# Mixture-of-experts routing on one Trainium2 core: one-hot comparisons for eight row tiles at once in 16 bits, a shorter ranking chain, eight row slots, 71 blocks

## Chip, cores and metric

The kernel runs on one core of one Trainium2 chip. The metric is the device time of one execution, in microseconds (us). TensorE (PE) multiplies matrices, VectorE (DVE) and GpSimd (POOL) and ScalarE (ACT) work elementwise, SyncE (SP) issues most DMAs; they meet only at semaphores.

## What is computed

Six layers in turn act on 8192 tokens (8 sequences of 1024) of 128 numbers each: a gated mixture of experts (m0), a gated scan (s0), the same mixture again (m1), a second kind of mixture (m2), a selective scan (s1) and that mixture once more (m3). The change touches the four mixtures. What matters of the reference, for the second kind:

```python
capacity = int(CAP_RATIO * N * K / E) + 1          # 2561 rows per expert
k_probs, k_idx = jax.lax.top_k(probs, K)           # two of eight experts
flat_e = k_idx.reshape(-1)
onehot = jax.nn.one_hot(flat_e, E, dtype=jnp.int32)
rank = take_along_axis(cumsum(onehot, axis=0) - 1, flat_e[:, None], axis=1)[:, 0]
keep = rank < capacity
buf = zeros((E, capacity, H)).at[flat_e, slot].add(dispatched)
h = silu(einsum('ech,ehf->ecf', buf, w1));  out_buf = einsum('ecf,efh->ech', h, w2)
```

In the gated kind (m0, m1) no row is dropped, and an expert is `silu(x @ W1a + b1a) * (x @ W1b + b1b) @ W2 + b2`.

## The kernel before

All 8192 tokens stay in SBUF as 64 tiles of 128 rows (`c.x`), handled in 16 groups of four (`GRP`, `NG`). A mixture (`moe`) has two halves.

The first half is the routing. Per group, DVE computes the mean and variance, ACT normalises the four tiles into a slot of `xs` (L502; there are four slots, and ACT waits at L499 until the store of the group that had the slot has landed), SP stores the slot to `rows_in` in DRAM (L569), PE transposes it (L452) and computes eight logits per token (L458). SP issues its DMAs in program order: at group 2 (L584) it issues the loads of all expert weights before it stores that group. When the logits of all groups are there, DVE picks the two best experts (L337 to L349) and PE counts them with two 16-bit matmuls (L469, L470). Then comes the ranking (L366 to L412), a chain of short DVE instructions on 128x512 (all tokens by eight experts), 128x64 (all tokens) and 128x8 arrays, in which each waits for the one before (`link`). It gives each of the 16384 choices a row number: its rank within its expert plus the start of that expert, rounded up to blocks of 256 rows. Then the inverse is made (the sort loop, L416 to L427 and L472 to L487): for each group, 128x128 and 128x144 one-hot matrices in 32 bits are made of the low and high part of the row numbers, DVE making nine, ACT four and POOL three, and PE multiplies eight pairs of them into `src_ps`, where each row finds the token it comes from. There are two slots for the one-hot matrices, so a group waits until the group before the last has been multiplied (`marks_used`). After the loop DVE finds the expert of each block (L428 to L433) and writes the sources as integers (L436 to L442).

The second half runs over 72 blocks of 256 rows: POOL gathers the rows from DRAM (L636), PE transposes and multiplies them (L664, L670, L676, L686), DVE copies the block's expert weights (L760, L765), and the result goes back to DRAM, scattered to token order in m0 and m1 (L643) and by rows in m2 and m3 (L826). The number of blocks does not depend on the data; the ones beyond the last expert work on padding.

`add_and_store` (L1806) ends the program: POOL gathers the outputs of m3, DVE adds them, SP stores them.

## Time and profile before

The median of three runs is 3682.92 us (3680.77 to 3684.62). The profiled execution took 3686.03 us, with a span of 3683.9 us from the first to the last instruction.

| stage | us from the span's start | what it is |
|---|---|---|
| m0 routing | 12 to 157 | groups to 82, choice to 93, ranking to 108, sort loop to 156 |
| m0 blocks | 157 to 568 | PE busy 97% |
| m1 routing, blocks | 925 to 1078, to 1490 | as m0 |
| m2 routing, blocks | 1495 to 1675, to 1955 | groups fed by fetched rows of m1 |
| m3 routing, blocks | 3095 to 3235, to 3515 | as m2, without the fetches |
| end | 3518 to 3684 | gather, add, store |

| engine | busy us | share of the span |
|---|---|---|
| PE | 2759.8 | 75% |
| DVE | 2230.1 | 61% |
| POOL | 2187.1 | 59% |
| ACT | 1574.8 | 43% |

The chain that ended last leads back only through the last stage. All layers follow one another behind barriers, so each stage has to be read by itself. In the rows below, a number in square brackets is the idle time of the engine before the instruction, and behind the arrow stands what ended it.

### The profile page before, as it was taken

How to read it: one execution, taken by the hardware profiler on the slowest of the kernel's cores; microseconds unless marked ns; L12 is line 12 of the kernel's file. 1: busy time of each engine (PE TensorE's matmuls, PEld its weight loads, DVE VectorE, ACT ScalarE, POOL GpSimd, SP SyncE). 2: the span in 40 equal slices, each digit the busy share in tenths (PEclk: the TensorE clock that was granted, in tenths of full speed). 3: DMA queues.
4: the chain of work that ended last, by engine and by line, in shares of the span. 5: the costliest groups of instructions: out<-in, count | busy, mean ns of one | idle time of the engine just before them, and what ended most of it. 6: DMA issues, size and time to landing. Idle time of an engine off the chain costs nothing. (4 is left out here: it accounts for less than half of the span.)

```text
span 3683.9 us, 48898 instructions
## 1 busy us (share of the span) xinstructions
PE 2759.8 (75%) x13060; PEld 2000.6 (54%) x13064; DVE 2230.1 (61%) x4405; ACT 1574.8 (43%) x2906; POOL 2187.1 (59%) x1931
## 2 busy tenths in 40 slices
PE   4699995998569999348995567767867865599910
PEld 4599983444459898348993223323322323589910
DVE  3766653555375565584331698999989987733322
ACT  4433334553443333243333566456556633433300
POOL 0577771321057777335553888988988684455567
PEclk9999997888589999569997799899999998699955
DMA  6011122000401111512222678778877875022222
GB/s 166 11 47 47 46 43 57 23 23 0 121 10 47 45 47 44 149 35 53 70 69 52 222 268 284 257 266 277 274 256 271 277 258 187 23 57 71 69 67 78
DMA packets 287279, 430.21 MB, mean 117 GB/s; under 512 B 58620, under 2 KB 196639, under 8 KB 287168
## 3 DMA queue, kind: packets, MB, share of 16 engines
q1 hardware_dynamic: 251328, 357.61, 29.5%
q0 software_dynamic: 35840, 71.39, 8.3%
q8 instruction: 37, 0.61, 0.1%
q14 instruction: 74, 0.61, 0.1%
HBM read 368.04 MB, written 62.91 MB: 117 GB/s over the span
## 5 line engine op out<-in xcount | busy, mean ns | idle before, releaser
L636 POOL DMA_INDIRECT m_rows<-rows_in,m_source x576 | 560.3, 973 | 370.1 <-PE m_T_ps L664 217.8
L1516 PE MATMUL s_y_ps<-s_prod,ident 128*128 128x512 f32 x1024 | 550.6, 666 | 277.2 <-DVE s_prod L1785 276.9
L1778 DVE TENSOR_TENSOR_SCAN s_dA<-s_dA,s_dBu 128x1024 f32<-128x1024 f32 x256 | 586.2, 2290 | 143.6 <-POOL s_dBu L1476 70.8
L1476 POOL TENSOR_TENSOR s_dBu<-s_du,s_B_row 128x1024 f32<-128x1024 f32 x256 | 602.6, 2358 | 101.8 <-DVE s_dA L1778 94.1
L670 PE MATMUL m_A_ps<-m_rowsT,m_own 128*128 128x256 f32 x2304 | 576.8, 383 | 2.0 <-ACT m_rowsT L718 1.1
L686 PE MATMUL m_Y_ps<-m_own,m_hid 128*128 128x128 f32 x4608 | 562.2, 275 | 3.6 <-issue 3.6
L686 PEld LDWEIGHTS m_Y_ps<-m_own,m_hid 128*128 128x128 f32 x4608 | 537.3, 192 | 5.7 <-issue 5.6
L1516 PEld LDWEIGHTS s_y_ps<-s_prod,ident 128*128 128x128 f32 x1024 | 192.3, 205 | 598.1 <-DVE s_prod L1785 404.9
L670 PEld LDWEIGHTS m_A_ps<-m_rowsT,m_own 128*128 128x128 f32 x2304 | 420.3, 193 | 49.4 <-ACT m_rowsT L718 1.9
L1606 ACT ACTIVATE s_dA<-s_delta,s_decay 128x1024 f32<-128x1024 f32 x256 | 285.6, 1118 | 337.4 <-DVE s_prod L1785 330.8
L728 ACT ACTIVATE m_act_a<-m_A_ps,m_own 128x256 f32<-128x256 f32 x576 | 241.4, 470 | 434.9 <-PE m_A_ps L670 303.4
L643 POOL DMA_INDIRECT rows_by_token<-m_y_sb,m_target x288 | 307.2, 1067 | 138.3 <-issue 100.9
L777 DVE SCALAR_TENSOR_TENSOR m_hid<-m_B_ps,m_own,m_act_a 128x256 f32<-128x256 f32 x576 | 250.7, 476 | 179.9 <-ACT m_act_a L728 165.4
L1785 DVE TENSOR_TENSOR s_prod<-s_dA,s_C_row 128x1024 f32<-128x1024 f32 x256 | 313.3, 1224 | 8.3
L733 ACT ACTIVATE m_hid<-m_A_ps 128x512 f32<-128x512 f32 x288 | 171.9, 597 | 329.4 <-PE m_A_ps L670 329.4
L676 PE MATMUL m_B_ps<-m_rowsT,m_own 128*128 128x256 f32 x1152 | 297.4, 381 | 0.0
L760 DVE COPY m_own<-m_packs 128x1032 f32 (+1 forms) x288 | 170.1, 591 | 127.2 <-issue 76.2
L791 DVE COPY m_y_sb<-m_Y_ps 128x256 f32<-128x256 f32 x144 | 61.2, 425 | 294.6 <-PE m_Y_ps L686 294.6
L676 PEld LDWEIGHTS m_B_ps<-m_rowsT,m_own 128*128 128x128 f32 x1152 | 220.1, 191 | 30.3
L477 PE MATMUL m_src<-m_is_high,m_is_low 128*128 128x144 f32 x1024 | 151.9, 306 | 100.0 <-DVE m_is_high L424 90.0
L477 PEld LDWEIGHTS m_src<-m_is_high,m_is_low 128*128 128x128 f32 x1024 | 139.2, 203 | 115.4 <-DVE m_is_high L424 87.3
L551 POOL COPY m_low_now<-m_low 128x4 f32 (+1 forms) x64 | 12.2, 191 | 309.8 <-DVEq L414 280.9
(228 smaller groups left out, 3994.4 us busy)
## 6 DMA issues: line engine op xcount, KB each, us to landing
s_B_row<-s_bc_rows SPq DMA_DIRECT2D x256, 512.0 KB, 5.3
s_C_row<-s_bc_rows SPq DMA_DIRECT2D x256, 512.0 KB, 5.4
rows_out<-m_y_sb SPq DMA_DIRECT2D x144, 128.0 KB, 1.8
rows_in<-m_xs SPq DMA_DIRECT2D x64, 256.0 KB, 2.3
m_rows<-rows_in,m_source POOLq DMA_INDIRECT x576
s_got<-rows_by_token SPq DMA_DIRECT2D x16, 512.0 KB, 5.2
m_got<-rows_by_token SPq DMA_DIRECT2D x32, 256.0 KB, 4.1
rows_by_token<-m_y_sb,m_target POOLq DMA_INDIRECT x288, 2.3
```

What stands on the lines that cost most here:

```text
L477: ins = nc.tensor.matmul(src_ps[:, :], is_low[:, slot, j % 2, j // 2, :], is_high[:, slot, j, :], start=isinstance(g, int) and g == 0 and ...
L636: pool.indirect_dma_start(rows[:, b % 2, r, :], None, c.rows_in, bass.IndirectOffsetOnAxis(source[:, 2 * b + r:2 * b + r + 1], 0)).then_in ...
L643: pool.indirect_dma_start(c.rows_by_token, bass.IndirectOffsetOnAxis(target[:, 2 * b + r:2 * b + r + 1], 0), y_sb[:, b % 2, r, :], None, b ...
L670: ins = nc.tensor.matmul(A_ps[h][:, j, :], own[:, slot, W1A + f * P:W1A + (f + 1) * P], rowsT[:, slot, :], start=True, stop=True)
L676: ins = nc.tensor.matmul(B_ps[h][:, j, :], own[:, slot, W1B + f * P:W1B + (f + 1) * P], rowsT[:, slot, :], start=True, stop=True)
L686: ins = nc.tensor.matmul(Y_ps[slot][:, r, :], hid[:, slot, f, at(r, P)], own[:, slot, W2 + f * D:W2 + (f + 1) * D], start=(f == 0), stop=( ...
L777: ins = nc.vector.scalar_tensor_tensor(out=hid[:, slot, f, :], in0=B_ps[h][:, j, :], scalar=own[:, slot, B1B + f:B1B + f + 1], in1=act_a[: ...
L1476: nc.gpsimd.tensor_tensor(dBu[q % RING][:, :], du[s % 2][:, h, :], B_row[q % RING][:, :], ALU.mult).then_inc(dBu_ready, 1)
L1516: ins = nc.tensor.matmul(y_ps[:, at(cc, 512)], c.ident[:, :], prod[q % 2][:, at(cc, 512)], start=(n == 0), stop=(n == NS - 1))
L1606: nc.scalar.activation(dA[q % 2][:, :], delta[s % 2][:, h, :], ACT.Exp, scale=decay[:, h, n:n + 1]).then_inc(dA_ready, 1)
L1778: nc.vector.tensor_tensor_scan(dA[q % 2][:, :], dA[q % 2][:, :], dBu[q % RING][:, :], 0.0, ALU.mult, ALU.add).then_inc(scanned, 1)
L1785: nc.vector.tensor_tensor(prod[q % 2][:, :], dA[q % 2][:, :], C_row[q % RING][:, :], ALU.mult).then_inc(prod_ready, 1)
```

## The change

- Slots of `xs`: eight in place of four (`DEEP`).
- Counting: the order of the moving operand is by expert and then tile, read with a step of eight 16-bit elements; the matrix `earlier` holds -1 so that the sum of the two gives the rank.
- Ranking: one scan over all experts that starts anew where `restart` is zero, in place of eight; the start of the expert is added before the choice is picked, so that two instructions per choice go; both choices are split into low and high part together. In m2 and m3 a dropped choice gets a number from 32768 on, which matches no row; `keep`, the weights and the row to fetch back are worked out after the sort loop.
- Sort loop: `is_high` and `is_low` of eight tiles are one DVE instruction each (1152 and 1024 elements per partition, 16 bits, the tile innermost). A one-hot matrix no longer carries the token number; `is_high` is multiplied by the tile number (DVE in even groups, POOL in odd ones) and by the row within the tile (ACT). PE multiplies with 288 columns, both parts together, reading both operands with a step of eight 16-bit elements. The loop is written out. Afterwards the two parts are put together by two more DVE instructions.
- Blocks: 71 in place of 72, which is still enough for any split of the choices.
- Constants are made at the start for the new shapes (1024 and 1152 elements per partition where there were 128 and 144).

```diff
-NBLK = 2 * TOK // BLK + E
+NBLK = (2 * TOK + E * (BLK - 1)) // BLK
 ROWS = NBLK * BLK
 CAP = int(1.25 * TOK * 2 / E) + 1
+DROPPED = 32768.0
...
-            link(nc.gpsimd.memset(c.before[:, :], 1.0))
-            link(nc.gpsimd.affine_select(out=c.before[:, :], in_=c.before[:, :], compare_op=ALU.is_gt,
-                                         fill=0.0, base=0, pattern=[[1, P]], channel_multiplier=-1))
+            link(nc.gpsimd.memset(c.earlier[:, :], 0.0))
+            link(nc.gpsimd.affine_select(out=c.earlier[:, :], in_=c.earlier[:, :], compare_op=ALU.is_gt,
+                                         fill=-1.0, base=0, pattern=[[1, P]], channel_multiplier=-1))
...
+            link(nc.gpsimd.memset(c.restart[:, :, :], 1.0))
+            link(nc.gpsimd.memset(c.restart[:, :, 0:1], 0.0))
...
-            link(nc.gpsimd.iota(low_i[:, :], pattern=[[1, P]], base=0, channel_multiplier=0))
-            link(nc.gpsimd.iota(high_i[:, :], pattern=[[P, ROWS // P]], base=0, channel_multiplier=0))
-            link(nc.gpsimd.iota(code_i[:, :, :], pattern=[[TOK, 2], [P, NT]], base=1, channel_multiplier=1))
+            link(nc.gpsimd.iota(low_i[:, :, :], pattern=[[1, P], [0, 2 * GRP]], base=0, channel_multiplier=0))
+            link(nc.gpsimd.iota(high_i[:, :, :], pattern=[[1, ROWS // P], [0, 2 * GRP]], base=0, channel_multiplier=0))
+            link(nc.gpsimd.iota(tile_i[:, :, :, :], pattern=[[GRP, NG], [NT, 2], [1, GRP]], base=0, channel_multiplier=0))
...
+        DEEP = 8
         with ExitStack() as rc:
             def rsb(name, shape, dt=F32):
                 return rc.enter_context(nc.sbuf_tensor(f"{tag}_{name}", shape, dt))
-            xs = rsb("xs", [P, 4, GRP, D])
+            xs = rsb("xs", [P, DEEP, GRP, D])
...
+            is_low = rsb("is_low", [P, 2, P, 2 * GRP], BF16)
+            is_high = rsb("is_high", [P, 2, ROWS // P, 2 * GRP], BF16)
+            coded = rsb("coded", [P, 2, 2, ROWS // P, 2 * GRP], BF16)
...
-            src_ps = rc.enter_context(nc.psum_tensor(f"{tag}_src", [P, ROWS // P], F32))
+            src_ps = rc.enter_context(nc.psum_tensor(f"{tag}_src", [P, 2, ROWS // P], F32))
...
-                for e in range(E):
-                    link(nc.vector.tensor_tensor_scan(cum[:, e, :], c.ones_f[:, :], tot3[:, :, e], 0.0,
...
+                link(nc.vector.tensor_tensor_scan(cum[:, :, :].rearrange("p e t -> p (e t)"), c.restart[:, :, :].rearrange("p e t -> p (e t)"),
+                                                  tot_ps[:, :], 0.0, ALU.mult, ALU.add))
                 if gated:
-                    link(nc.vector.tensor_copy(cnt[:, :], cum[:, :, NT - 1]))
+                    link(nc.vector.tensor_scalar(cnt_i[:, :], cum[:, :, NT - 1], float(BLK - 1), None, ALU.add))
                 else:
-                    link(nc.vector.tensor_scalar(cnt[:, :], cum[:, :, NT - 1], float(CAP), None, ALU.min))
...
+                    link(nc.vector.tensor_scalar(cnt_i[:, :], cum[:, :, NT - 1], float(CAP), float(BLK - 1), ALU.min, ALU.add))
+                link(nc.vector.tensor_tensor(cum[:, :, :], cum[:, :, :], by_expert[0], ALU.add))
                 link(nc.vector.tensor_scalar(cnt_i[:, :], cnt_i[:, :], BLK.bit_length() - 1, BLK.bit_length() - 1,
                                              ALU.logical_shift_right, ALU.logical_shift_left))
                 link(nc.vector.tensor_copy(cnt[:, :], cnt_i[:, :]))
                 link(nc.vector.tensor_tensor_scan(run_end[:, :], c.ones_f[:, 0:E], cnt[:, :], 0.0, ALU.mult, ALU.add))
                 link(nc.vector.tensor_tensor(run_base[:, :], run_end[:, :], cnt[:, :], ALU.subtract))
+                if not gated:
+                    link(nc.vector.tensor_scalar(over[:, :, :], cum[:, :, :], float(CAP), DROPPED, ALU.is_ge, ALU.mult))
+                    link(nc.vector.tensor_tensor(cum[:, :, :], cum[:, :, :], over[:, :, :], ALU.add))
+                link(nc.vector.tensor_tensor(place[:, :, :], cum[:, :, :].rearrange("p e t -> p t e"),
+                                             run_base[:, :].unsqueeze(1).to_broadcast([P, NT, E]), ALU.add))
                 for k in range(2):
-                    link(nc.vector.tensor_tensor(t8[:, :, :], oh[k][:, :, :], u8[:, :, :], ALU.mult))
-                    link(nc.vector.tensor_reduce(rank[:, :], t8[:, :, :], AX.X, ALU.add))
...
+                    link(nc.vector.tensor_tensor(t8[:, :, :], oh[k][:, :, :], place[:, :, :], ALU.mult))
+                    link(nc.vector.tensor_reduce(pos[:, k, :], t8[:, :, :], AX.X, ALU.add))
+                link(nc.vector.tensor_copy(pos_i[:, :, :], pos[:, :, :]))
+                link(nc.vector.tensor_scalar(high_i[:, :, :], pos_i[:, :, :], P.bit_length() - 1, None, ALU.logical_shift_right))
+                link(nc.vector.tensor_scalar(low_i[:, :, :], pos_i[:, :, :], P - 1, None, ALU.bitwise_and))
+                link(nc.vector.tensor_copy(high[:, :, :, :], high_i[:, :, :].rearrange("p k (g j) -> p g k j", j=GRP)))
+                link(nc.vector.tensor_copy(low[:, :, :, :], low_i[:, :, :].rearrange("p k (g j) -> p g k j", j=GRP)))
+                def spread_over(v, n):
+                    return v.rearrange("p k j -> p (k j)").unsqueeze(1).to_broadcast([P, n, 2 * GRP])
+                for g in range(NG):
+                    wait(dve, marks_used, g - 1)
+                    nc.vector.tensor_tensor(is_high[:, g % 2, :, :], c.high[:, :, :], spread_over(high[:, g, :, :], ROWS // P),
+                                            ALU.is_equal).then_inc(high_ready, 1)
+                    nc.vector.tensor_tensor(is_low[:, g % 2, :, :], c.low[:, :, :], spread_over(low[:, g, :, :], P),
+                                            ALU.is_equal).then_inc(low_ready, 1)
+                    if g % 2 == 0:
+                        dve.wait_ge(high_ready, g + 1)
+                        nc.vector.tensor_tensor(coded[:, g % 2, 0, :, :], is_high[:, g % 2, :, :],
+                                                spread_over(c.tile_code[:, g, :, :], ROWS // P), ALU.mult).then_inc(tiles_coded[0], 1)
+                if not gated:
+                    for k in range(2):
+                        link(nc.vector.tensor_scalar(keep[:, :], pos[:, k, :], DROPPED, None, ALU.is_lt))
+                        link(nc.vector.tensor_tensor(weight[k][:, :], weight[k][:, :], keep[:, :], ALU.mult))
                 for k in range(2):
-                    link(nc.vector.tensor_copy(low[k][:, :], put_i[k][:, :]))
-                    link(nc.vector.tensor_scalar(put_i[k][:, :], put_i[k][:, :], bits, bits,
...
+                    link(nc.vector.tensor_scalar(get_i[k][:, :], pos[:, k, :], float(ROWS - 1), None, ALU.min))
...
+                value, code, second, padding = (found[:, i, :] for i in range(4))
+                link(nc.vector.tensor_scalar(value, src_ps[:, 0, :], float(P), None, ALU.mult))
+                link(nc.vector.tensor_tensor(value, value, src_ps[:, 1, :], ALU.add))
+                link(nc.vector.tensor_scalar(code, value, -1.0, 0.0, ALU.add, ALU.max))
+                link(nc.vector.tensor_scalar(second, code, float(TOK), float(-TOK), ALU.is_ge, ALU.mult))
...
-                ch = chosen[:, :, :].rearrange("p t e -> p (t e)")
-                nc.tensor.matmul(pre_ps[:, :], c.before[:, :], ch, start=True, stop=True)
...
+                ch = chosen[:, :, :].rearrange("p t e -> p e t")
+                nc.tensor.matmul(by_expert[0], c.earlier[:, :], ch, start=True, stop=True)
+                nc.tensor.matmul(by_expert[1], c.ones_bf[:, :], ch, start=True, stop=True).then_inc(counted, 1)
+                for g in range(NG):
+                    pe.wait_ge(low_ready, g + 1)
+                    pe.wait_ge(tiles_coded[g % 2], g // 2 + 1)
+                    pe.wait_ge(rows_coded, g + 1)
                     for j in range(2 * GRP):
-                        ins = nc.tensor.matmul(src_ps[:, :], is_low[:, slot, j % 2, j // 2, :], is_high[:, slot, j, :],
-                                               start=isinstance(g, int) and g == 0 and j == 0,
-                                               stop=last and j == 2 * GRP - 1)
+                        ins = nc.tensor.matmul(src_ps[:, :, :], is_low[:, g % 2, :, j], coded[:, g % 2, :, :, j],
+                                               start=(g == 0 and j == 0), stop=(g == NG - 1 and j == 2 * GRP - 1))
                     ins.then_inc(marks_used, 1)
-                sort(0, 0)
-                sort(1, 1)
...
...
-                    wait(act, transposed, g - 3)
-                    wait(act, xs_stored[g % 4], g // 4 * 16)
+                    wait(act, transposed, g - DEEP + 1)
+                    wait(act, xs_stored[g % DEEP], g // DEEP * 16)
...
-                act.wait_ge(parts_known, 1)
...
+                for g in range(NG):
+                    act.wait_ge(high_ready, g + 1)
+                    nc.scalar.activation(coded[:, g % 2, 1, :, :], is_high[:, g % 2, :, :], ACT.Copy,
+                                         scale=c.row_code[:, 0:1]).then_inc(rows_coded, 1)
...
-                pool.wait_ge(parts_known, 1)
...
+                for g in range(1, NG, 2):
+                    pool.wait_ge(high_ready, g + 1)
+                    nc.gpsimd.tensor_tensor(coded[:, 1, 0, :, :], is_high[:, 1, :, :],
+                                            c.tile_code[:, g, :, :].rearrange("p k j -> p (k j)").unsqueeze(1).to_broadcast([P, ROWS // P, 2 * GRP]),
+                                            ALU.mult).then_inc(tiles_coded[1], 1)
...
-                with pe.Fori(0, (NBLK - 4) // 2) as i:
+                with pe.Fori(0, (NBLK - 3) // 2) as i:
                     step(i * 2 + 2, 0)
                     step(i * 2 + 3, 1)
-                step(NBLK - 2, 0)
-                step(NBLK - 1, 1, last=True)
-                down(NBLK - 1, 1)
+                step(NBLK - 1, 0, last=True)
+                down(NBLK - 1, 0)
```

## Rows read from the trace of the kernel before

**Rows 1.** Busy time by stage: start:end, length, engines, PEclk granted, DMA share, GB/s.

```profile
93.10:108.40 15.30, 0.00 (x0) 0.00 (x0) 13.87 (x38) 0.04 (x1) 0.01 (x1) 1.00 0.00 0
...
3095.00:3168.30 73.30, 42.60 (x207) 41.25 (x206) 38.22 (x192) 37.36 (x91) 27.77 (x64) 0.52 0.40 115
```

**Rows 2.** ACT in order of time: start, us, what; m0, m1, m2, m3.

```profile
53.76 1.65 ACT L502 ACTIVATE m_xs<-x_res,m_shift,m_rstd 128x128 f32<-128x128 f32 x4 [21.43 <-DMA rows_in<-m_xs]
...
974.46 1.65 ACT L502 ACTIVATE m_xs<-x_res,m_shift,m_rstd 128x128 f32<-128x128 f32 x4 [20.97 <-DMA rows_in<-m_xs]
...
984.27 1.65 ACT L502 ACTIVATE m_xs<-x_res,m_shift,m_rstd 128x128 f32<-128x128 f32 x4 [0.48 <-DVE m_shift L300]
...
1541.70 1.65 ACT L502 ACTIVATE m_xs<-x_res,m_shift,m_rstd 128x128 f32<-128x128 f32 x4 [12.93 <-DVE m_own_shift L304]
...
3125.27 1.65 ACT L502 ACTIVATE m_xs<-x_res,m_shift,m_rstd 128x128 f32<-128x128 f32 x4 [8.04 <-DMA rows_in<-m_xs]
```

**Rows 3.** SP's queue in order of time, m1.

```profile
944.73 14.32 SPq L182 DMA_DIRECT2D m_packs<-in_L_ffn_W  x4
...
969.70 28.52 SPq L569 DMA_DIRECT2D rows_in<-m_xs  x14
```

**Rows 4.** DVE in order of time, m2's groups.

```profile
1538.89 2.31 DVE L275 SCALAR_TENSOR_TENSOR x_res<-m_got,weight,x_res 128x128 f32<-128x128 f32 x8 [10.36 <-DMA m_got<-rows_by_token]
```

**Rows 5.** DVE in order of time, ranking and first one-hot, m0 then m2.

```profile
93.12 2.53 DVE L367 TENSOR_TENSOR_SCAN m_cum<-ones_f,m_tot 128x64 f32<-128x64 f32 x8
...
97.13 1.03 DVE L372 TENSOR_TENSOR m_u<-m_u,m_cum 128x512 f32<-128x512 f32 x1
...
98.41 0.17 DVE L378 TENSOR_SCALAR m_cnt<-m_cnt 128x8 f32<-128x8 f32 x1
...
99.64 0.69 DVE L386 TENSOR_TENSOR m_t<-m_oh,m_u 128x512 f32<-128x512 f32 x1
...
108.41 0.29 DVE L421 TENSOR_SCALAR m_is_low<-low,m_low 128x128 f32<-128x128 f32 x1
...
1607.76 2.53 DVE L367 TENSOR_TENSOR_SCAN m_cum<-ones_f,m_tot 128x64 f32<-128x64 f32 x8
...
1626.17 0.29 DVE L421 TENSOR_SCALAR m_is_low<-low,m_low 128x128 f32<-128x128 f32 x1
```

**Rows 6.** DVE at the end of m0's sort loop and at the first block.

```profile
154.43 0.31 DVE L436 TENSOR_SCALAR m_is_high<-m_src 128x144 f32<-128x144 f32 x1
...
157.59 0.70 DVE L760 COPY m_own<-m_packs 128x1032 f32 x1 [1.56 <-issue]
```

**Rows 7.** PE in m0's sort loop, last group; x16 are eight matmuls.

```profile
151.72 2.23 PE L477 MATMUL m_src<-m_is_high,m_is_low 128*128 128x144 f32 x16 [0.27 <-DVE m_is_high L424]
```

**Rows 8.** All engines in order of time, one step of s1.

```profile
3039.33 1.22 DVE L1785 TENSOR_TENSOR s_prod<-s_dA,s_C_row 128x1024 f32<-128x1024 f32 x1
3039.47 2.35 POOL L1476 TENSOR_TENSOR s_dBu<-s_du,s_B_row 128x1024 f32<-128x1024 f32 x1 [1.00 <-DVE s_dA L1778]
3040.47 2.29 DVE L1778 TENSOR_TENSOR_SCAN s_dA<-s_dA,s_dBu 128x1024 f32<-128x1024 f32 x1
...
3040.61 1.98 PE L1516 MATMUL s_y_ps<-s_prod,ident 128*128 128x512 f32 x4 [1.23 <-DVE s_prod L1785]
...
3040.65 1.12 ACT L1606 ACTIVATE s_dA<-s_delta,s_decay 128x1024 f32<-128x1024 f32 x1 [2.34 <-DVE s_prod L1785]
```

**Rows 9.** PE groups by line: xcount, busy us, mean ns, idle before.

```profile
L470 PE MATMUL m_tot<-m_chosen,ones_bf 128*128 128x512 bf16 x4 | 2.5, 634 | 48.2 <-DVE m_chosen L349 48.2
```

**Rows 10.** PE in order of time, two blocks of m0, two of m3.

```profile
501.19 0.38 PE L664 MATMUL m_T_ps<-ident,m_rows 128*128 128x128 f32 x2
...
506.65 0.38 PE L664 MATMUL m_T_ps<-ident,m_rows 128*128 128x128 f32 x2
...
3440.13 0.38 PE L664 MATMUL m_T_ps<-ident,m_rows 128*128 128x128 f32 x2
...
3443.86 0.38 PE L664 MATMUL m_T_ps<-ident,m_rows 128*128 128x128 f32 x2
```

164 lines of the change are left out of this document (45 added, 119 removed).

## The prediction

> **What bounds the kernel now.** I began with the busy slices of the page. They show PE near full in four stretches (the blocks of the mixtures) and no engine full in the routing ahead of each. The chain that ended last reaches back only through the last stage, which the change leaves alone, so I asked for the busy time by stage. In the ranking only DVE works, 13.87 of 15.30 us, and the DMA engines do nothing [rows 1]: whatever is cut from that chain comes off the end. The instructions in order of time then gave the rest. ACT, which sets the pace of the groups, stood still for 21.43 us in m0, 20.97 in m1 and 8.04 in m3 until a store of an older group had landed [rows 2]; SP had queued that store behind the weight loads [rows 3]. In m2 ACT waited 12.93 us for DVE instead, and DVE 10.36 us for fetched rows [rows 2, 4]. The sort loop takes 154.43 - 108.41 = 46.0 us from its first one-hot to the first closing instruction, on DVE, ACT, POOL and PE together [rows 5, 6]. In the blocks PE sets the pace.
>
> **Eight slots.** ACT does a group in (984.27 - 974.46) / 4 = 2.45 us [rows 2]. With four slots it stops after group 5, because group 6 needs the slot of group 2, whose store waits behind the loads. With eight it stops after group 9: four more groups, 9.8 us, move under the wait in m0 and in m1, and 11 us of the wait remain there, since the loads are no faster. In m3 the wait was 8.04 us, less than four groups, so all of it goes. Behind the waiting ACT instruction are the copies for PE, so PE moves with it. In m2 the wait is another one and nothing is gained. The stores then come in a burst; SP issued 14 in 28.52 us [rows 3], which was still at ACT's pace, so I cost the burst at nothing; if a store took over 2.45 us, it would show as a new ACT wait. Sum: 9.8 + 9.8 + 8.0 = 27.6 us less.
>
> **Ranking.** An instruction on 512 elements takes 0.69 us and one on 8 takes 0.17; with the step to the next I count 0.73 and 0.21. Reading across the experts makes the 0.69 a 1.03 [rows 5]. Eight scans of 64 take 2.53 us, one of 1024 takes 2.29 [rows 5, 8]; between the two, one of 512 takes 1.22. The new chain in m0: scan 1.25, five small ones 1.05, the add of the counts 0.73, the place with its crossing read 1.07, four on 512 elements 2.92, and five on 128 elements, for which I take 0.30 each by the 0.31 of a 144-element one [rows 6], 1.5. That is 8.5 us against 108.41 - 93.12 = 15.3: 6.8 us less. In m2 and m3 two more on 512 elements make it 10.0, against 1626.17 - 1607.76 = 18.4 [rows 5]: 8.4 less. All on the path. Sum: 2 x 6.8 + 2 x 8.4 = 30.4 us less.
>
> **Sort loop.** *DVE.* No row has a two-input instruction on 16-bit operands. At one element per step it follows the 0.69 for 512 and 1.22 for 1024 [rows 5, 8], so 1.36 us for 1152 elements. The fast end is the copy that took 0.70 us for 1032 elements [rows 6], so 0.76 for 1152 and 0.69 for 1024. The two-input row moves four bytes of each operand in a step; 1152 elements of two bytes that lie side by side are 576 such words, and that lands on the fast end. I take it: `is_high` 0.79 with its step, `is_low` 0.72, the multiplication in even groups 0.79.
>
> *POOL.* In odd groups it multiplies 1152 elements. By 2.35 us for 1024 [rows 8] that is 2.65. It could be as little as 1.26, which is ACT's rate [rows 8], if 16 bits help there.
>
> *PE.* A group was eight matmuls in 16 pieces in 2.23 us, so 0.129 us a piece of 144 columns at two cycles each [rows 7]. A 16-bit matmul on 512 columns took 0.634 us [rows 9] where the granted clock was near half [rows 1]; at 1.2 GHz two cycles a column would be 0.85, so 16-bit columns take one. A matmul of 288 columns then costs the same 0.129 and a group 1.2 us. But each column is now read 16 bytes from the last. The only price of such a read is DVE's 1.03 for 0.69 [rows 5], which without the 0.16 of fixed cost is 1.64 times per element. I take that: 0.206 us a matmul, 1.8 us a group. One cycle gives 1.2, two cycles 2.15.
>
> *The period.* An odd group can start only when the odd group before it has been multiplied. So two groups take at least `is_high` 0.76 + POOL 2.65 + PE 1.8 + three handovers. DVE to POOL took 0.17 (a scan ended at 3039.30, POOL began at 3039.47) and DVE to PE 0.06 (3040.55 to 3040.61) [rows 8]; 0.3 in all. That is 5.5 us. DVE needs 3.8 for its five instructions and PE 3.3; ACT needs 1.26 for each group, by 1.12 for 1024 [rows 8], and ends before POOL. The first odd group starts 2.3 us in, the last is multiplied after 2.3 + 8 x 5.5 = 46.3 us. DVE's work behind the loop fits under that in m0 and m1; in m2 and m3 the weights that were moved behind it end at 46.6. Before, it was 46.0 in m0 and as much elsewhere within 0.3 us. So the loop gains nothing by this sum, and two more closing instructions at 0.34 [rows 6] add 0.7: 1.0 us more per stage, 4.0 in all. The loop's other end: with one cycle a column the period is 4.9, and 18 us less in all; with two it is 5.86, and 12 more.
>
> *Beside the sum.* DVE's product and scan of s1, with two SBUF inputs each, ran during POOL's multiplication, and that took 2.35 us all the same [rows 8]. The Trainium skill (SBUF — State Buffer, "SBUF: two separate sides") says that such a DVE instruction and a GpSimd one that reads SBUF exclude each other for the whole instruction; the trace does not agree, and the rule is a rival below. And by the page VectorE: DVE Perf Modes, "The perf-mode tier table", 16-bit `tensor_tensor` runs at two elements per cycle, an estimate of 0.75 us for 1152; no row here shows that.
>
> **The rest.** Blocks: one less at 506.65 - 501.19 = 5.46 us in m0 and m1 and 3443.86 - 3440.13 = 3.73 in m2 and m3 [rows 10], 18.4 us less. Counting: two matmuls now read with a step; by the 1.64 above each adds 0.27 us at 1.2 GHz, partly under the weights that DVE works out meanwhile; I take 1 us in all, 0 to 2. The constants grow by two arrays of some 1100 elements on POOL and DVE, an estimate of 3 to 5 us in a row, under the first load of tokens; 0, up to 1 if that cover is short.
>
> **Sum.** -27.6 - 30.4 + 4.0 - 18.4 + 1 = -71.4 us. Against the profiled 3686.03 that is 3614.6; the median of the runs lies 3.1 lower, so 3611.5.
>
> **Rivals.**
> - POOL is faster in 16 bits (1.26): period 4.1, 10 us less per stage, 3571. Nothing in the trace speaks for it.
> - DVE makes one element per step. Then DVE sets the period, 2 x 1.39 + 2 x 1.26 + 1.39 = 6.7, and a stage takes 10.6 more: 3654. For it: every two-input row here has that rate.
> - DVE and POOL exclude each other: 3.8 + 2.65 = 6.5 per pair, 8 more per stage, 3643. Against it: [rows 8].
> - The slots bring nothing, because the stores, bunched, hold ACT again: 3639.
> - Slower than before: the stepped read costs PE the time, not the ratio, that it costs DVE. (1.03 - 0.16) / 512 = 1.7 ns an element [rows 5] is 0.49 us for 288 columns, 0.5 a matmul, and PE sets the period: 16 x 0.5 = 8.0 us. The loop takes 66.3, 20 more in each stage: 3691.5. It decides from 0.48 us a matmul on. For it: this is the only stepped read in the trace. Against it: PE's clock and port are others. The Trainium skill (SBUF — State Buffer, "Specifications (TRN2)") has lines of 16 bytes that want two hits each for full bandwidth, and each column here is a line of its own; it gives no size, and no row of PE shows one.
>
> **How the numbers follow.** Forecast 60% (3593 to 3623 with the ends of the stepped read); faster POOL 9%; DVE at one per step 9%; exclusion 8%; slots without effect 7%; slow stepped read 7%. The range 3575 to 3652 takes in the forecast, the exclusion, the slots and the near halves of two others. 0.2%, about what a measurement can tell from no change, is 7.4 us: only the last rival gets there, so faster 93%, the same 2%, slower 5%.
>
> **What would show it.** ACT's wait for the store at 11 us in m0 and m1 and gone in m3; 8.5 and 10.0 us from the scan to the first `is_high`; `is_high` at 0.76; POOL's product at 2.65; a matmul of the sort loop each 0.13 (one cycle), 0.21 or 0.25; two groups in 5.5 us, POOL's product in every chain; 71 blocks. The prediction is wrong if DVE idles in the loop for PE rather than for POOL's groups, or if `is_high` takes 1.36.

## The result: 0.4% slower, and the profile after

The changed kernel takes 3697.02 us (median; 3692.5 to 3699.8) beside 3682.19 us of the kernel before on the same chip: ratio 1.0037, 95% interval 1.0025 to 1.0049. The profiled execution took 3695.92 us, its span 3694.1 us, so 10.2 us more span than the 3683.9 of before. I had forecast 71.4 us less.

First the busy time by stretch: the sort loop of m0 before the change, then the four sort loops after it, each from the first one-hot instruction to the first closing instruction (columns: stretch; length; busy time of PE, PEld, DVE, ACT and POOL with the count of instructions; granted clock as a share of the full 2.4 GHz; DMA share; GB/s).

```profile
108.40:154.40 46.00, 37.66 (x256) 34.49 (x256) 42.59 (x153) 30.39 (x80) 33.44 (x64) 1.00 0.00 0
```

```profile
92.32:159.60 67.28, 64.99 (x128) 18.58 (x128) 31.53 (x52) 19.89 (x16) 19.68 (x8) 1.00 0.00 0
1012.04:1079.34 67.30, 65.02 (x128) 18.55 (x128) 31.55 (x51) 19.89 (x16) 19.71 (x8) 0.50 0.00 0
1619.57:1686.86 67.29, 65.00 (x128) 18.58 (x128) 32.38 (x56) 19.88 (x16) 19.69 (x8) 0.50 0.00 0
3180.20:3247.47 67.27, 64.99 (x128) 18.55 (x128) 32.38 (x56) 19.89 (x16) 19.69 (x8) 0.50 0.00 0
```

Three things matter. A loop takes 67.3 us, where before it took 46.0 [rows 5, 6]. PE is busy for 65.0 of them, DVE for less than half, POOL for less than a third; before, DVE was the busiest. And the first loop ran at a granted clock of 1.00 (2.4 GHz), the other three at 0.50 (1.2 GHz), and they are equally long: what PE does here does not go by its clock. A matmul costs 64.99 / 128 = 0.508 us, 1.79 ns for each of 284 columns.

The groups by line say the same from the other side (busy us, mean ns of one; then the idle time before them and what ended it), first PE's group of the kernel before, then those of the changed kernel:

```profile
L477 PE MATMUL m_src<-m_is_high,m_is_low 128*128 128x144 f32 x1024 | 151.9, 306 | 100.0 <-DVE m_is_high L424 90.0
```

```profile
L464 PE MATMUL m_src<-m_coded,m_is_low 128*128 128x284 bf16 x512 | 260.0, 687 | 44.5 <-ACT m_coded L507 44.5
...
L398 DVE TENSOR_TENSOR m_is_high<-high,m_high 128x1136 bf16<-128x1136 bf16 x64 | 48.0, 749 | 134.7 <-PE m_src L464 134.6
...
L457 PE MATMUL m_tot<-m_chosen,ones_bf 128*128 128x512 bf16 x4 | 4.3, 1078 | 0.0
```

DVE stands still for 134.6 us ahead of `is_high`, for PE. Before, the counting matmul of 512 columns took 634 ns [rows 9]; now that its operand is read across the experts, 16 bytes from one column to the next, it takes 1078 ns (the other counting matmul 1060). The mean of one sort matmul, 687 ns, is longer than the 508 from one to the next, since they overlap.

Single instructions in order of time, DVE and POOL in m0 (start, us, instruction; in brackets the idle time before it), and ACT's wait for a slot in m0 and m1:

```profile
94.92 0.68 DVE L400 TENSOR_TENSOR m_is_low<-low,m_low 128x1024 bf16<-128x1024 bf16 x1
98.77 0.75 DVE L398 TENSOR_TENSOR m_is_high<-high,m_high 128x1136 bf16<-128x1136 bf16 x1 [3.17 <-PE m_src L464]
...
152.26 2.46 POOL L520 TENSOR_TENSOR m_coded<-m_is_high,tile_code 128x1136 bf16<-128x1136 bf16 x1 [5.65 <-DVE m_is_high L398]
...
152.69 2.30 DVE L412 TENSOR_SCALAR get<-m_pos 128x64 int32<-128x64 f32 x2
...
159.60 0.30 DVE L421 TENSOR_SCALAR m_found<-m_src 128x142 f32<-128x142 f32 x1 [1.75 <-PE m_src L464]
```

```profile
54.15 1.65 ACT L481 ACTIVATE m_xs<-x_res,m_shift,m_rstd 128x128 f32<-128x128 f32 x4 [12.01 <-DMA rows_in<-m_xs]
...
973.87 1.65 ACT L481 ACTIVATE m_xs<-x_res,m_shift,m_rstd 128x128 f32<-128x128 f32 x4 [11.77 <-DMA rows_in<-m_xs]
```

`is_high` on 1136 elements takes 0.75 us: the fast end that I took, where one element per step would be 1.36. The waits for a store fell from 21.43 and 20.97 us [rows 2] to 12.01 and 11.77, and the one of m3 is gone. Also, two short `TENSOR_SCALAR` of 64 elements lasted 2.30 us together, beside POOL's product, where such an instruction took 0.20 in the kernel before; the experiments on GpSimd beside VectorE take that up.

Where the 10.2 us come from, by the same five points in both traces (start of the logits' copy, scan, first one-hot, first closing instruction, first copy of the blocks), summed over m0, m1, m2 and m3 (us; the forecast of +1.2 for the loops is the 4.0 of the sum less the 2.8 of the closing instructions):

| stretch | before | after | difference | forecast |
|---|---|---|---|---|
| all outside the routing (slots, blocks) | | | -46.8 | -27.6 - 18.4 |
| logits to scan (counting) | 51.9 | 54.3 | +2.4 | +1 |
| scan to first one-hot (ranking) | 67.4 | 35.4 | -32.0 | -30.4 |
| the four sort loops | 184.7 | 269.1 | +84.5 | +1.2 |
| closing | 10.8 | 12.9 | +2.1 | +2.8 |
| sum | | | +10.2 | -71.4 |

All of the miss is in one line of the table.

### The profile page after: what moved, and what is told of

It is laid out like the page before. It is cut to its first block and busy times, and to the rows that moved or that the text cites. A ratio compares the mean times of both kernels' runs of the same rounds, so it can differ in the third digit from the quotient of the medians.

```text
span 3694.1 us, 45149 instructions
## 1 busy us (share of the span) xinstructions
PE 2844.7 (77%) x12432; PEld 1913.7 (52%) x12432; DVE 2150.1 (58%) x3886; ACT 1525.3 (41%) x2634; POOL 2129.3 (58%) x1697
## 5 line engine op out<-in xcount | busy, mean ns | idle before, releaser
L601 POOL DMA_INDIRECT m_rows<-rows_in,m_source x568 | 552.0, 972 | 372.3 <-PE m_T_ps L629 211.4
L635 PE MATMUL m_A_ps<-m_rowsT,m_own 128*128 128x256 f32 x2272 | 567.1, 382 | 2.1 <-ACT m_rowsT L682 1.1
L651 PE MATMUL m_Y_ps<-m_own,m_hid 128*128 128x128 f32 x4544 | 554.4, 275 | 3.6 <-issue 3.6
L651 PEld LDWEIGHTS m_Y_ps<-m_own,m_hid 128*128 128x128 f32 x4544 | 529.8, 192 | 5.7 <-issue 5.6
L520 POOL TENSOR_TENSOR m_coded<-m_is_high,tile_code 128x1136 bf16<-128x1136 bf16 x32 | 78.8, 2462 | 397.8 <-DVE m_is_high L398 397.8
L464 PE MATMUL m_src<-m_coded,m_is_low 128*128 128x284 bf16 x512 | 260.0, 687 | 44.5 <-ACT m_coded L507 44.5
L464 PEld LDWEIGHTS m_src<-m_coded,m_is_low 128*128 128x128 bf16 x512 | 74.3, 146 | 233.4 <-issue 181.7
```

Source lines behind the costliest of these rows:

```text
L464: ins = nc.tensor.matmul(src_ps[:, :, :], is_low[:, g % 2, :, j], coded[:, g % 2, :, :, j], start=(g == 0 and j == 0), stop=(g == NG - 1 a ...
L601: pool.indirect_dma_start(rows[:, b % 2, r, :], None, c.rows_in, bass.IndirectOffsetOnAxis(source[:, 2 * b + r:2 * b + r + 1], 0)).then_in ...
L635: ins = nc.tensor.matmul(A_ps[h][:, j, :], own[:, slot, W1A + f * P:W1A + (f + 1) * P], rowsT[:, slot, :], start=True, stop=True)
L651: ins = nc.tensor.matmul(Y_ps[slot][:, r, :], hid[:, slot, f, at(r, P)], own[:, slot, W2 + f * D:W2 + (f + 1) * D], start=(f == 0), stop=( ...
```

## The experiments

Theory: the read of the moving operand with a step of 16 bytes sets the pace of the sort loop. Rivals: the matmuls are slow for another reason (two-part destination, unrolled code, waits); or the step of the weights is what costs; and, within the theory, whether the price goes by column, by instruction, or by bytes passed over. Eight of the runs below (all but those of halves, 32 bytes, 32-bit inputs, the changed kernel again and the two stretches) were on two other chips, on which the kernel before takes 3841 and 3845 us, so there ratios are compared, not times. Six runs were a single execution each: weights in pairs, 32-bit inputs, halves, 32 bytes and the two stretches; of them the traces are read, not the times.

**Pairs instead of eights.** The one-hot tensors are laid out so that PE steps over 4 bytes; the vector work is the same. `WL` and `WH` are the tiles side by side in `is_low` (the weights) and in `coded` (the moving operand); the cut shows `is_low` and the matmul alone.

```
+WL, WH = 2, 2
...
-            is_low = rsb("is_low", [P, 2, P, 2 * GRP], BF16)
+            is_low = rsb("is_low", [P, 2, 2 * GRP // WL, P, WL], BF16)
...
-                        ins = nc.tensor.matmul(src_ps[:, :, :], is_low[:, g % 2, :, j], coded[:, g % 2, :, :, j],
+                        ins = nc.tensor.matmul(src_ps[:, :, :], is_low[:, g % 2, j // WL, :, j % WL], coded[:, g % 2, :, j // WH, :, j % WH],
```

> The changed kernel with its one-hot tensors laid out in pairs of tiles instead of eights (the innermost dimension is 2): the vector instructions write as many elements in as many instructions, and TensorE reads both operands with a step of 4 bytes where it was 16. Theory 1 (the matmuls are slow by the 16-byte step): a matmul falls from 0.508 us to 0.12 to 0.24 us (284 columns at either clock level), the period of two groups becomes 0.75 + 2.46 + 8 x 0.2 + 0.3 = 5.1 us instead of 8.1, each stage's loop about 42 us instead of 67.3, and the time is 3697 - 4 x 25 = 3597 us. Theory 2 (it is not the step: 16-bit matmuls into a destination of two parts, the unrolled code, or the waits ahead of each group make them slow): nothing changes in a matmul, 3697 us. A third outcome: the vector instructions lose two elements per cycle with so short an innermost dimension: is_high takes 1.2 us instead of 0.75.

Measured: ratio 0.9802 (0.9786 to 0.9818), where the changed kernel has 1.0037. The groups of this kernel:

```profile
L465 PE MATMUL m_src<-m_coded,m_is_low 128*128 128x284 bf16 x512 | 110.4, 384 | 101.0 <-ACT m_coded L508 54.0 <-POOL m_coded L521 47.0
...
L399 DVE TENSOR_TENSOR m_is_high<-high,m_high 128x1136 bf16<-128x1136 bf16 x64 | 80.3, 1255 | 22.4 <-PE m_src L465 21.7
```

PE's 260.0 us became 110.4, and it now waits for the others. So the layout alone is worth 2.4%, and theory 2 falls. But the loops take 45.5 to 46.5 us, not 42, and `is_high` has a mean of 1255 ns instead of 749. That is not the loss of two elements per cycle that I had as a third outcome: most of them take 0.74 us, and some far longer. The order of time shows which (PE's eight matmuls of a group among them):

```profile
105.20 2.05 PE L465 MATMUL m_src<-m_coded,m_is_low 128*128 128x284 bf16 x8 [0.74 <-ACT m_coded L508]
...
105.78 2.46 POOL L521 TENSOR_TENSOR m_coded<-m_is_high,tile_code 128x1136 bf16<-128x1136 bf16 x1 [2.61 <-DVE m_is_high L399]
...
107.29 1.56 DVE L399 TENSOR_TENSOR m_is_high<-high,m_high 128x1136 bf16<-128x1136 bf16 x1 [0.99 <-PE m_src L465]
...
110.43 0.75 DVE L399 TENSOR_TENSOR m_is_high<-high,m_high 128x1136 bf16<-128x1136 bf16 x1 [0.32 <-PE m_src L465]
...
111.26 2.46 POOL L521 TENSOR_TENSOR m_coded<-m_is_high,tile_code 128x1136 bf16<-128x1136 bf16 x1 [3.02 <-DVE m_is_high L399]
...
112.19 2.13 DVE L399 TENSOR_TENSOR m_is_high<-high,m_high 128x1136 bf16<-128x1136 bf16 x1 [0.41 <-PE m_src L465]
...
113.82 1.19 PE L465 MATMUL m_src<-m_coded,m_is_low 128*128 128x284 bf16 x8 [1.67 <-POOL m_coded L521]
...
115.51 0.74 DVE L399 TENSOR_TENSOR m_is_high<-high,m_high 128x1136 bf16<-128x1136 bf16 x1
```

The first of these POOL products ends at 108.24, the comparison at 108.85; the second ends at 113.72, the comparison at 114.32. Both comparisons end 0.6 us after POOL's product, whatever their start: they wait for its end. The one at 110.43, with POOL idle, takes 0.75. In the changed kernel no `is_high` is longer than 0.75 us, because PE kept DVE waiting for longer.

How much of the 45.5 us is that wait? POOL's products begin 5.48 or 5.07 us apart (105.78, 111.26, 116.32), so two groups take about what the sum of the prediction had, 5.5 us, with no wait in it. The longer periods are those in which PE's group took 2.05 us, at a granted clock of 0.50: POOL's product, PE's group and the next `is_high` follow one another there, and the held comparison lies beside them. In the shorter ones PE took 1.19 us, at 1.00, and was done at 115.01, but `is_high` began only at 115.51, behind the DVE instructions that the held comparison had put off. By this the wait costs under 0.5 us in about half of the periods, an estimate of 2 us a loop; what holds the loop is POOL's product, 2.46 us in every two groups.

**Which operand.** Only the moving operand in pairs, then only the weights.

```
-WL, WH = 2, 2
+WL, WH = 8, 2
```

> As the changed kernel, but only the moving operand (coded, with is_high) is laid out in pairs, so a step of 4 bytes; the weights (is_low) are still read with a step of 16 bytes. If the step of the moving operand costs the time (my theory: 284 columns against 128 in the weights, and the weight load, 146 ns each, lies beside the matmul before it): as with both in pairs, a matmul of 0.12 to 0.24 us, about 3597 us. If the step of the weights costs it: 0.508 us a matmul as before, 3697 us.

```
-WL, WH = 2, 2
+WL, WH = 2, 8
```

> The other half: only the weights (is_low) in pairs, a step of 4 bytes, the moving operand (coded) still with a step of 16 bytes. Theory of the moving operand: 0.508 us a matmul as in the changed kernel, 3697 us. Theory of the weights: 0.12 to 0.24 us a matmul, about 3597 us.

Measured: 0.9805 (0.9789 to 0.9821) and loops of 45.6 to 47.1 us for the moving operand alone; for the weights alone loops of 66.5 us and one time of 3848.0 us beside 3841.4. The moving operand is nearly the whole of it: PE is busy for 117.1 us with it alone in pairs, for 110.4 with both and for 256.9 with the weights alone, so the step of the weights is worth 3 to 7 us in 512 matmuls, about 0.01 us each.

**How the price grows.** Fours, a step of 8 bytes:

```
-WL, WH = 2, 2
+WL, WH = 4, 4
```

> Both operands laid out in fours: a step of 8 bytes. If the cost grows with the bytes stepped over, a matmul lies midway, 0.25 to 0.33 us, the period is 0.75 + 2.46 + 8 x 0.29 + 0.3 = 5.8 us, the loop about 48 us, the time 3697 - 4 x 19 = 3620 us. If it is a threshold at 16 bytes, 0.12 to 0.24 us and about 3597 us as with pairs; if any step costs the full price, 0.508 us and 3697 us.

Measured: 0.9843 (0.9826 to 0.9859). Busy time by stretch, its first and third loop:

```profile
93.26:140.98 47.72, 33.99 (x128) 14.76 (x128) 38.86 (x51) 19.88 (x16) 19.68 (x8) 0.78 0.00 0
1719.87:1768.56 48.69, 33.97 (x128) 14.87 (x128) 39.70 (x55) 19.89 (x16) 19.67 (x8) 0.61 0.00 0
```

33.99 / 128 = 0.266 us a matmul, 0.93 ns a column, at both mixes of the clock: midway, as by the bytes passed over, not a threshold. The pairs did go by the clock, 1.19 / 8 = 0.149 us at 1.00 and 2.05 / 8 = 0.256 at 0.50. So a step of 8 bytes nearly doubles a matmul at the full clock and adds next to nothing at half of it.

**Columns or instructions; 32 bytes.** Two matmuls of 142 columns each for one of 284; and `coded` spread to 32 bytes a column.

```
-                        ins = nc.tensor.matmul(src_ps[:, :, :], is_low[:, g % 2, :, j], coded[:, g % 2, :, :, j],
+                        for half in range(2):
+                            ins = nc.tensor.matmul(src_ps[half][:, 0:ROWS // P], is_low[:, g % 2, :, j], coded[:, g % 2, half, :, j],
```

> The changed kernel (step of 16 bytes) with each matmul of 284 columns made as two of 142, into two banks: twice the instructions, the same columns. If the stepped read costs its time per column (1.79 ns): 0.254 us each, the group still 4.06 us, the loop 67.3 us, no change. If it is a cost of each instruction (a table of descriptors, a restart of the read): 0.5 us each, 8.1 us a group, loops of 130 us, 250 us more.

```
-            coded = rsb("coded", [P, 2, 2, ROWS // P, 2 * GRP], BF16)
+            coded = rsb("coded", [P, 2, 2, ROWS // P, 4 * GRP], BF16)
```

> The changed kernel with coded spread out so that TensorE's columns lie 32 bytes apart instead of 16 (the eight values of a column and then eight unused ones); is_high, is_low and the number of columns as they were. The pairs, fours and eights gave 0.149, 0.264 and 0.508 us for 284 columns, 0.52, 0.93 and 1.79 ns a column at steps of 4, 8 and 16 bytes. If the time follows the bytes passed over: 3.6 ns a column, 1.02 us a matmul, 8.1 us a group, loops of 130 us and 250 us more. If it stops growing once each column has 16 bytes of its own: 0.508 us, the loop 67.3 us, no change but for the vector writes.

Measured, the matmul groups of the two:

```profile
L465 PE MATMUL m_src<-m_coded,m_is_low 128*128 128x142 bf16 x1024 | 264.4, 438 | 44.6 <-ACT m_coded L508 44.6
```

```profile
L464 PE MATMUL m_src<-m_coded,m_is_low 128*128 128x284 bf16 x512 | 264.2, 695 | 44.5 <-ACT m_coded L507 44.5
```

Twice the instructions: 264.4 us busy instead of 260.0. Twice the step: 264.2. Loops of 68.4 us in both, single times of 3703.6 and 3696.6 us beside 3682.7 of the kernel before. The price goes by column, and from 16 bytes on it no longer grows. They ran beside the changed kernel itself, with no edit:

> The changed kernel as it is, beside the others of this group, so that the kernels in pairs can be set against it on one chip. Its first runs gave a ratio of 1.0037 to the kernel before; the same is expected, 1.002 to 1.005, since the four loops of 67.3 us each lie 21 us over those of before and the rest of the change gives back about 74 us.

which again had 1.0040 (1.0026 to 1.0054).

**The steps by themselves.** A stretch of matmuls of 512 columns put in front of the kernel before, with DVE and POOL forms side by side in the same stretch.

```
+STEPS_BF = (1, 2, 3, 4, 6, 8, 12, 16, 32)
...
+                for s in STEPS_BF:
+                    v = col[:, 0:512 * s].rearrange("p (n s) -> p n s", s=s)[:, :, 0]
+                    for j in range(8):
+                        nc.tensor.matmul(banks[k % 4][:, :], ha[:, 0:P], v, start=True, stop=True).then_inc(pe_done, 1)
```

> The kernel before with a stretch put in behind the constants that computes nothing the kernel needs; its time is longer by that stretch and says nothing, only the stretch is read. TensorE: eight matmuls in a row for each of nine steps of a 16-bit moving operand (2 to 64 bytes, 512 columns), for weights with a step of 16 bytes, and for four steps of a 32-bit one. By 4, 8, 16 and 32 bytes so far (0.52, 0.93, 1.79, 1.8 ns a column): 6 bytes 0.7, 12 bytes 1.3, 24 and 64 bytes 1.8 ns, whatever the clock; the weights' step costs the matmul nothing. If the read goes by whole lines instead, 12 bytes costs 1.8 and 6 bytes 0.93. VectorE beside GpSimd: seven forms on 1024 elements, each started 0.4 to 1 us after a GpSimd instruction of 2.35 us, and again with GpSimd idle; four forms on GpSimd. Theory A (VectorE waits where its own instruction writes or reads 16 bits, or is a one-input form): 32-bit two-input forms and the scan are as long beside GpSimd as alone, the 16-bit ones and tensor_scalar last until GpSimd's end and their own time more, whatever GpSimd does. Theory B (it waits where GpSimd's instruction has 16-bit operands): all forms wait beside these and none beside the 32-bit one. Theory C (the operand spread by a step of zero makes it): only those forms wait.

The weight loads (PEld), one for each matmul, show the pitch, the time from one matmul to the next. Here eight loads in one row with a step of 4 bytes, then two from each of four groups, six matmuls apart: steps of 8, 12 (begins at 55.08), 16 and 32 bytes.

```profile
46.52 1.67 PEld L1945 LDWEIGHTS t_o<-t_col,t_ha 128*128 128x128 bf16 x8 [0.25 <-issue]
...
51.24 0.12 PEld L1945 LDWEIGHTS t_o<-t_col,t_ha 128*128 128x128 bf16 x1 [0.34 <-issue]
...
53.95 0.11 PEld L1945 LDWEIGHTS t_o<-t_col,t_ha 128*128 128x128 bf16 x1 [0.34 <-issue]
...
55.08 0.12 PEld L1945 LDWEIGHTS t_o<-t_col,t_ha 128*128 128x128 bf16 x1 [0.56 <-issue]
...
59.13 0.12 PEld L1945 LDWEIGHTS t_o<-t_col,t_ha 128*128 128x128 bf16 x1 [0.55 <-issue]
...
60.70 0.12 PEld L1945 LDWEIGHTS t_o<-t_col,t_ha 128*128 128x128 bf16 x1 [0.78 <-issue]
...
66.10 0.12 PEld L1945 LDWEIGHTS t_o<-t_col,t_ha 128*128 128x128 bf16 x1 [0.78 <-issue]
...
75.07 0.13 PEld L1945 LDWEIGHTS t_o<-t_col,t_ha 128*128 128x128 bf16 x1 [0.79 <-issue]
...
80.58 0.12 PEld L1945 LDWEIGHTS t_o<-t_col,t_ha 128*128 128x128 bf16 x1 [0.79 <-issue]
```

The first row is seven pitches and a last load of 0.10 us, so 1.57 / 7; the others are 2.71 / 6, 4.05 / 6, 5.40 / 6 and 5.51 / 6 us. Divided by 512 columns, and with the steps of 6, 24 and 64 bytes read in the same way:

| step of a 16-bit column, bytes | 4 | 6 | 8 | 12 | 16 | 24 | 32 | 64 |
|---|---|---|---|---|---|---|---|---|
| ns a column | 0.44 | 0.66 | 0.88 | 1.32 | 1.76 | 1.74 | 1.79 | 1.67 |

From 4 to 16 bytes it is 0.11 ns for each byte from one column to the next, then flat. At 4 bytes that is hardly more than what columns side by side cost: in a second pass the 16 matmuls with steps of 2 and 4 bytes took 3.55 us together, 0.43 ns a column, at a granted clock of 1.00. The other pitches were the same in the second pass; that of 8 bytes is 0.45 us in both, at 1.00, and that of 16 bytes is 0.90 us here at 0.50 and by the column the same in m0 of the changed kernel at 1.00. A 32-bit matmul shows two weight loads, and from one to the next it took 0.43 us at a step of 4 bytes, 0.45 at 8, 0.90 at 16 and 0.92 at 32, at 1.00: from 8 bytes on the price goes by the step in bytes, not by the type, and below it 32-bit columns have a price of their own that is higher. Weights read with a step of 16 bytes and contiguous columns took 0.43 us at a granted clock of 0.50. The first matmuls of the stretch, contiguous in both, took 0.43 us too; the view gives 1.00 for them, but 512 columns in 0.43 us is one column per cycle of 1.2 GHz. Twelve bytes and whole lines: I had that as an alternative (1.8 ns), and it falls.

**GpSimd beside VectorE.** Theory: DVE waits for POOL's product; so without that product the long comparisons go.

```
-                    if g % 2 == 0:
-                        dve.wait_ge(high_ready, g + 1)
-                        nc.vector.tensor_tensor(coded[:, g % 2, 0, :, :, :], is_high[:, g % 2, :, :, :],
...
+                    dve.wait_ge(high_ready, g + 1)
+                    nc.vector.tensor_tensor(coded[:, g % 2, 0, :, :, :], is_high[:, g % 2, :, :, :],
...
-                for g in range(1, NG, 2):
-                    pool.wait_ge(high_ready, g + 1)
-                    nc.gpsimd.tensor_tensor(coded[:, 1, 0, :, :, :], is_high[:, 1, :, :, :],
```

> The layout in pairs, and GpSimd does no multiplication: VectorE multiplies by the tile codes for every group (737 ns each). Theory 1 (VectorE's next comparison waits for GpSimd's multiplication to end, as its 1.56 and 2.13 us instead of 0.74 in the pairs kernel suggest): the long comparisons are gone, is_high is 0.74 us in every group, a group costs VectorE 0.67 + 0.60 + 0.66 = 1.93 us, two slots give (0.75 + 1.24 + 2.0) / 2 = 2.0 us a group, each loop about 35 us instead of 45.5, 42 us less than the pairs kernel, ratio 0.969. Theory 2 (the long comparisons wait for something else, as for TensorE's reads): they stay, VectorE has 0.66 us more a pair, the loop is 46 to 50 us, ratio 0.980 to 0.986.

Measured: ratio 0.9691 (0.9675 to 0.9707). Its first loop by stretch, and the group of `is_high`:

```profile
92.72:127.21 34.49, 21.04 (x128) 12.18 (x128) 33.79 (x59) 19.88 (x16) 0.00 (x0) 1.00 0.00 0
```

```profile
L399 DVE TENSOR_TENSOR m_is_high<-high,m_high 128x1136 bf16<-128x1136 bf16 x64 | 48.0, 750 | 1.5 <-PE m_src L464 1.3
```

All 64 comparisons take 0.75 us, DVE works 33.8 of 34.5 us, and the loops are 34.5 to 35.6 us. More work on DVE made the loop 11 us shorter, because POOL's help had cost more than it gave. This run takes away two things at once, the long comparisons and POOL's 2.46 us in the chain of every two groups, where DVE needs 0.74. By the estimate from the pairs kernel the wait is about 2 of the 11 us and the product's own length the rest; no run has one without the other. This version beats both kernels, by 3.1% of the kernel before.

Four slots instead of two, on top of it:

```
+SL = 4
...
-                    wait(dve, marks_used, g - 1)
-                    nc.vector.tensor_tensor(is_high[:, g % 2, :, :, :], c.high[:, :, :, :], spread_over(high[:, g, :, :], ROWS // P, WH),
+                    wait(dve, marks_used, g - SL + 1)
+                    nc.vector.tensor_tensor(is_high[:, g % SL, :, :, :], c.high[:, :, :, :], spread_over(high[:, g, :, :], ROWS // P, WH),
```

> As the kernel in pairs in which VectorE multiplies for every group, with four slots for is_high, is_low and coded instead of two. If VectorE sets the loop (1.93 us a group) it is 16 x 1.93 + 3.5 = 34.4 us, almost as with two slots, ratio 0.968 to 0.969. If the chain comparison, ACT's copy, matmuls through two slots sets it, four slots give more: what is over 34.4 us with two slots goes. If TensorE sets it (8 matmuls of 0.237 us at the lower clock, 1.9 us a group) nothing changes either.

Measured: 0.9690 (0.9674 to 0.9706), loops of 34.1 to 35.1 us. Four slots give 0.4 us a loop; DVE sets it.

Does only the two-elements-per-cycle form wait? The same pairs kernel with 32-bit inputs of `is_high`:

```
-            high = rsb("high", [P, NG, 2, GRP], BF16)
+            high = rsb("high", [P, NG, 2, GRP])
...
-        c.high = sb("high", [P, 2 * GRP // WH, ROWS // P, WH], BF16)
+        c.high = sb("high", [P, 2 * GRP // WH, ROWS // P, WH])
```

> The kernel in pairs (GpSimd still multiplies for the odd groups) with the two inputs of the is_high comparison in 32 bits instead of 16; its output stays 16 bits wide, so the instruction has one element per step, about 1.24 us instead of 0.74. Theory 1 (only the 16-bit form at two elements per cycle waits for GpSimd's instruction): none of them is longer than 1.3 us and the loop is VectorE's 2 x (1.17 + 0.60) + 0.66 = 4.2 us a pair or the chain comparison 1.24, GpSimd 2.46, TensorE 1.9 and handovers 0.3 = 5.9 us a pair, about 49 us. Theory 2 (every two-input instruction of VectorE waits): those that start beside a GpSimd multiplication last until its end and 1.1 us more, up to 2.6 us, and the loop is over 50 us.

```profile
102.96 2.46 POOL L521 TENSOR_TENSOR m_coded<-m_is_high,tile_code 128x1136 bf16<-128x1136 bf16 x1 [3.79 <-DVE m_is_high L399]
...
103.87 2.74 DVE L399 TENSOR_TENSOR m_is_high<-high,m_high 128x1136 bf16<-128x1136 f32 x1 [0.39 <-PE m_src L465]
```

Loops of 53.3 and 54.3 us; alone it takes 1.33 us, beside POOL 2.74: it waits too. Here the wait does set the loop. POOL's products are 6.25 us apart in all of it, and that is POOL's 2.46, 1.2 until the held comparison ends, and the three DVE instructions up to the next product. The waiting stood against [rows 8], where 32-bit products and scans ran beside POOL's product undisturbed. The stretch of matmuls above also held pairs of DVE and POOL instructions, which settle what waits: a POOL product, and DVE instructions started 0.45 us behind it.

```profile
51.77 2.40 POOL L1897 TENSOR_TENSOR t_pf<-t_ga,t_gb 128x1024 f32<-128x1024 f32 x1
...
52.22 3.04 DVE L1891 TENSOR_TENSOR t_dfh<-t_fa,t_fb 128x1024 bf16<-128x1024 f32 x1 [0.69 <-ACT t_aout L1935]
...
66.13 2.50 DVE L1894 TENSOR_SCALAR t_dts<-t_fa 128x1024 f32<-128x1024 f32 x1 [0.69 <-ACT t_aout L1935]
...
70.05 4.07 DVE L1895 TENSOR_TENSOR_SCAN t_dsc<-t_fa,t_fb 128x1024 f32<-128x1024 f32 x1 [0.69 <-ACT t_aout L1935]
...
113.10 1.89 POOL L1899 TENSOR_TENSOR t_pb<-t_ka,t_k 128x1024 bf16<-128x1024 bf16 x1
```

Alone the three DVE instructions take 1.23, 0.69 and 2.29 us: each was held for some 1.8 us, and ended its own time less 0.15 us behind POOL. All seven forms waited beside all three kinds of POOL product, with 32 or 16 bits, spread operand or not: theories A, B and C all fall. (POOL's own `TENSOR_SCALAR` of 2.77 us held them for 0.45 us only.) The last row is the form of the sort loop's product, by itself: 1.89 us for 1024 elements, an estimate of 2.10 for 1136, where it takes 2.46 in every loop. There each product begins 0.16 us into `is_low`, a DVE instruction with two SBUF inputs that has 0.52 us to go (105.62 and 105.78 in the pairs kernel). So the missing 0.36 us is most likely POOL waiting for DVE in its turn; no run shifts the two against each other to show it. What is different in s1 stands in the code and in no row:

```
        dA = [ps(f"dA{i}", SEQ) for i in range(2)]
```

`dA`, an input of both of s1's DVE instructions, lies in PSUM (`ps`), not in SBUF. The last run tried that by itself; the cut shows two of its four forms.

```
+                 lambda: tt(d["dfb"][:, :], psum_in[:, :], fb[:, :], ALU.add),
+                 lambda: nc.vector.tensor_tensor_scan(psum_out[:, :], psum_in[:, :], fb[:, :], 0.0, ALU.mult, ALU.add),
```

> The kernel before with a stretch that computes nothing it needs, as in the run before; only the stretch is read. Four forms of VectorE on 1024 elements, each started about 0.45 us after a GpSimd product of 2.35 to 2.4 us (32 bits, both inputs in SBUF), and again with GpSimd idle: the sum of two SBUF tiles; the sum of a PSUM tile and an SBUF tile; the scan with its first input and its output in PSUM, as in s1; a reduction with one SBUF input. If it is the place of the operands: the first lasts 1.95 us more beside GpSimd (3.05 instead of 1.1 to 1.2), the other three are as long as alone (1.2, 2.3 and 1.1 us, within 0.1). If it is something else in s1: the second and third last 3.0 and 4.1 us, like the first.

```profile
27.71 2.35 POOL L1895 TENSOR_TENSOR t_pf<-t_ga,t_gb 128x1024 f32<-128x1024 f32 x1
...
28.15 1.23 DVE L1891 TENSOR_TENSOR t_dfb<-t_psum_in,t_fb 128x1024 f32<-128x1024 f32 x1 [0.69 <-ACT t_aout L1930]
...
32.07 2.30 DVE L1892 TENSOR_TENSOR_SCAN t_psum_out<-t_psum_in,t_fb 128x1024 f32<-128x1024 f32 x1 [0.69 <-ACT t_aout L1930]
```

With one input in PSUM both are as long as alone (1.23 and 2.30 us), and so is a reduction of one SBUF tile (1.22). The control with two SBUF inputs started 1.83 us behind POOL here and was held for 0.37 us (1.60 for 1.23); the 1.8 us are those of the stretch before. So it is the place of the operands.

**Slots and blocks alone.** Each edit in the kernel before by itself.

```
-            xs = rsb("xs", [P, 4, GRP, D])
+            xs = rsb("xs", [P, 8, GRP, D])
```

> The kernel before with eight row slots instead of four, nothing else. My sum gave 27.6 us to this edit (9.8 in the first stage, 9.8 in the second, none in the third, 8.0 in the fourth): ratio 0.9925. If the slots only move the wait to the rows that arrive (12.01 us stand ahead of ACT's normalisation in the changed kernel's first stage), or if the earlier stores collide with the fetches of the fourth stage, half of it or less: ratio 0.996 to 1.000.

```
-NBLK = 2 * TOK // BLK + E
+NBLK = (2 * TOK + E * (BLK - 1)) // BLK
```

> The kernel before with 71 blocks instead of 72, nothing else. My sum gave 18.4 us, four times one block at the pitch of the block loop: ratio 0.9950. Rival: the last block runs in slot 0 on its own and the drain behind it is no shorter, half of that: ratio 0.9975.

Measured: 0.9930 (0.9914 to 0.9947) and 0.9940 (0.9922 to 0.9957). The slots give what the sum gave them, and the wait left in m0 is 11.89 us. The forecast of 0.9950 for the blocks lies within the interval, and the rival's 0.9975 outside it; the medians differ by 24.5 us, above my 18.4, and the other chip may have dearer blocks: that is not told apart. In the traces of the first chip 20.1 us are left for the blocks and the rest, when the three waits of the slots are taken from the 46.8.

## Why the prediction was wrong

**The step that failed: the price of PE's stepped read.** From one row (1.03 us where 0.69 was the contiguous price [rows 5]) I drew two prices, a ratio of 1.64 and a time of 1.7 ns an element. I put the ratio into the sum, 0.206 us a matmul, and left the time to a rival at 7%. The runs showed 0.508 us for 284 columns, 1.79 ns each: the time carries over from DVE to PE almost to the digit, the ratio does not. That it does so closely may be chance. DVE's row reads 32-bit elements 256 bytes apart, and no run shows one cause behind both prices. A ratio supposes that the stepped read slows in proportion to whatever the engine does otherwise. The four loops at two clock levels show the opposite, a rate of the read that PE's clock doesn't touch. The rival's whole chain held: period 8.1 us against its 8.0, loops of 67.3 against 66.3, time 3697.0 against 3691.5. My ground against it, that PE has another clock and port, was no number. With both prices equally likely, as one row warrants, the range would have had to reach 3692, and it ended at 3652. The Trainium skill (SBUF — State Buffer, "Specifications (TRN2)") has 16-byte lines that want two hits each for full bandwidth. The runs agree that 16 bytes is where the price stops growing; with two hits a line (8 bytes) a column still costs 0.88 ns where it is 0.44 at 4 bytes, so at the full clock the loss begins before that.

**A second step was wrong, hidden in the result: DVE and POOL.** I wrote that s1's product and scan have two SBUF inputs each, and set the exclusion at 8% on that ground. One input is in PSUM. The Trainium skill's rule (SBUF — State Buffer, "SBUF: two separate sides"), that a DVE instruction with two SBUF inputs and a GpSimd one that reads SBUF exclude each other for the whole instruction, is what the two stretches show beside a product of POOL, held by 1.8 us and not at all; beside POOL's `TENSOR_SCALAR` they show 0.45 us, so there "for the whole instruction" does not fit. I said that the trace disagreed; it only looked so. In the changed kernel this cost nothing in the loop, since DVE had 134.6 us of waiting for PE to hide it in. The price that I had put on it, 6.5 us for two groups, was wrong as well: with PE's read at a fair price the sum of the prediction gives 0.76 + 2.46 + 2.0 + 0.3 = 5.5 us, and the pairs kernel, wait and all, has 5.07 to 5.48. Most of the wait lies beside POOL's product, which is in the chain anyway; only with the comparison in 32 bits did it set the period, 6.25 us.

**What held.** `is_high` at 0.75 us for 0.76. POOL's product 2.46 for 2.65; by itself, though, the 16-bit form took 1.89 us for 1024 elements where the 32-bit one took 2.35 to 2.42, so the figure was near partly by luck, most likely with 0.36 us of waiting in it. Eight matmuls at one cycle a column 1.19 for 1.2 (the pairs kernel at the full clock). The sum counts 1.0 us a stage for the loops and closing of all four, although the working has 46.6 us for the loops of m2 and m3: 0.6 us left out, of no weight. Ranking 8.24 and 9.44 for 8.5 and 10.0. The slots: 9.4 us of wait less in m0, 9.2 in m1, all of the 8.0 in m3, nothing in m2; with the blocks, all outside the routing gave -46.8 for -46.0. Closing +2.1 for +2.8. Counting was mis-sized: +2.4 for +1, because the two matmuls became 1.06 and 1.08 us, 0.44 more, where I had added 0.27 to 0.63. Of the marks I had named for a wrong prediction, the first is the one that showed: DVE idles in the loop for PE, not for POOL's groups.

**What the forecast would have been with the two measured terms:** -46.0 - 30.4 + 1 + 2.8 for the rest, and 4 x (67.3 - 46.2) = +84.4 for the loops, +11.8 us, where the traces show +10.2.

## What to carry to other kernels

A tensor that PE reads as the moving operand wants its columns side by side; if a vector engine must write several tiles at once, let two of them alternate, not eight: the vector instructions cost the same (`is_high` 0.75 us in both) and a step of 4 bytes costs the matmul next to nothing. A second engine in the chain has to pay for its whole time there: POOL's 2.46 us for a product that DVE does in 0.74 made the loop 11 us longer. Where one row gives the price of an unseen thing both as a ratio and as a time, cost the change by both, and give the slower one as much chance as the other. Before a pair of rows is taken as proof that two engines don't disturb each other, look up in the code where each operand lies; no row says whether it is SBUF or PSUM.

## What the runs showed of the hardware

- PE's moving operand in 16 bits: 0.11 ns a column for each byte from one column to the next, from 4 bytes (0.44) to 16 (1.76), then 1.67 to 1.8 ns at any step up to 64 bytes. The price at 16 bytes is the same at a granted clock of 0.50 and 1.00 (67.3 us a loop at both), and that at 8 bytes the same at both mixes (0.93 ns). At 4 bytes the clock counts: eight matmuls of 284 columns took 1.19 us at 1.00 and 2.05 at 0.50. 32-bit columns took 0.43, 0.45, 0.90 and 0.92 us for each of two passes over 512 columns, at 4, 8, 16 and 32 bytes.
- The step of the weights costs about 0.01 us a matmul (PE busy for 117.1 us with a step of 16 bytes, 110.4 with 4).
- DVE's two-input 16-bit instruction keeps its pace (0.75 us for 1136 elements, where 32-bit inputs take 1.33) with an innermost dimension of only two elements and an operand spread over the rows.
- A DVE instruction with two SBUF inputs, or a `TENSOR_SCALAR`, that starts while a POOL product with SBUF inputs runs ends 0.55 us (own time 0.69) or 1.09 us (own time 1.23) after it, whenever it began; with one input in PSUM, or as a reduction, it isn't held (1.23 and 1.22 us). Behind a `TENSOR_SCALAR` of POOL (2.77 us) it is held for 0.45 us.
- POOL's product of 1136 elements is 2.46 us in every sort loop, where `is_low` is under way as it begins, and the same form by itself 1.89 us for 1024.
- The granted clock was 1.00 in m0's loop and 0.50 in the three others, where PE was busy for 97% of the time in all four; what decides between the two is not shown.
